# Tokens on partitions for the last expert sums: fp32 matmuls with the one-hots as stationary operand in place of two float32r passes, copies and transposes

## What is computed

```python
x = x + _L0_xattn_ref(_layernorm(x, axis=-1), ctx_1024, ...)
x = x + _L0_ffn_ref(_layernorm(x, axis=-1), L0_ffn_Wg, L0_ffn_W1, L0_ffn_W2)
...
expert_inputs = jnp.einsum('bnd,bnec->becd', token_inputs, dispatch)
h = jax.nn.gelu(jnp.einsum('becd,edh->bech', expert_inputs, W1))
expert_outputs = jnp.einsum('bech,ehd->becd', h, W2)
output = jnp.einsum('becd,bnec->bnd', expert_outputs, combine)
```

## Time and profile before

| | |
|---|---|
| median of 3 runs | 138.56 us (138.42 to 139.27) |
| the profiled execution | 138.64 us |
| its span | 136.9 us |
| busy in the span | PE 124.2 us (91%), DVE 93.6 us (68%), ACT 79.4 us (58%), POOL 33.6 us (25%) |
| granted TensorE clock, mean | 0.996 |

### The profile page before, as it was taken

One profiled execution on the slowest core, in us unless ns is written; L12 is line 12 of the kernel. 1 busy time (PEld: TensorE's weight loads), 2 busy tenths in 40 slices (PEclk: granted clock), 3 DMA queues, 4 the chain that ended last, 5 costly groups with the idle time before them and its releaser, 6 DMA issues.

```text
span 136.9 us, 2770 instructions
## 1 busy us (share of the span) xinstructions
PE 124.2 (91%) x1038; PEld 89.0 (65%) x1039; DVE 93.6 (68%) x304; ACT 79.4 (58%) x154; POOL 33.6 (25%) x54
## 2 busy tenths in 40 slices
PE   6999988999899998998978997699999999999950
PEld 2573843664664754754834943599999799987830
DVE  2797656996996996996997899974782041134751
ACT  1568383945855865765636678863694265315350
POOL 7633805005005005005000060027000065550000
PEclk9999999999999999999999999999999999999998
DMA  3989991000000000000000000000101201113115
GB/s 98 277 226 333 366 382 51 0 0 7 0 0 0 0 5 0 0 2 0 5 0 0 0 0 0 0 5 0 41 5 38 77 24 30 34 31 87 34 42 153
DMA packets 9197, 8.05 MB, mean 59 GB/s; under 512 B 601, under 2 KB 7028, under 8 KB 9184
## 3 DMA queue, kind: packets, MB, share of 16 engines
q1 hardware_dynamic: 8492, 7.28, 16.6%
q0 software_dynamic: 256, 0.40, 1.2%
q10 hardware_dynamic: 436, 0.20, 0.6%
HBM read 6.43 MB, written 1.57 MB: 58 GB/s over the span
## 4 chain that ended last, share of the span: by engine, by line
PE 71%; DVE 14%; ACT 9%; issue 3%; POOL 1%; ACTq 0%; DVEq 0%
PE ps L1302 11%; PE ps L1288 11%; PE ps L1144 6%; PE ps L1117 6%; PE ps L1136 5%; PE ps L1110 5%; PE ps L980 3%; PE ps L1314 3%; PE ps L1218 3%; ACT r_b L422 3%; PE ps L1063 3%; PE ps L1181 2%; PE ps L1093 2%; ACT z_b L436 2%; PE ps L1074 2%
## 5 line engine op out<-in xcount | busy, mean ns | idle before, releaser
L1144 PE MATMUL ps<-attn,VW 32*128 32x256 f32 x144 | 12.9, 426 | 3.5 <-DVE ps L712 2.0
L1288 PE MATMUL ps<-h,W_t 128*128 128x128 f32 x128 | 15.9, 279 | 0.0
L1288 PEld LDWEIGHTS ps<-h,W_t 128*128 128x128 f32 x128 | 15.0, 192 | 0.5 <-issue 0.3
L429 ACT ACTIVATE ps<-ps,half_b 128x512 f32<-128x512 f32 x12 | 7.9, 660 | 12.7 <-PE ps L1117 12.7
L1136 PE MATMUL ps<-h,whhT 128*128 128x256 f32 x48 | 13.7, 405 | 0.0
L1117 PE MATMUL ps<-h,whhT 128*128 128x256 f32 x48 | 13.3, 398 | 0.0
L346 POOL DMA_INDIRECT y_tok<-y_rows,row_of x8 | 8.3, 1034 | 18.9 <-DMA y_rows<-y_sb 14.1
L1144 PEld LDWEIGHTS ps<-attn,VW 32*128 32x128 f32 x144 | 5.6, 182 | 10.6 <-DVE ps L712 4.4
L1110 PE MATMUL ps<-h,whhT 128*128 128x256 f32 x48 | 11.7, 384 | 0.0
L422 ACT ACTIVATE r_b<-ps,half_b 128x512 f32<-128x512 f32 x12 | 7.6, 684 | 7.1 <-PE ps L1144 7.1
L712 DVE SCALAR_TENSOR_TENSOR ps<-r_b,ps 128x512 f32<-128x512 f32 x12 | 7.8, 693 | 5.1 <-ACT r_b L422 5.1
(11 more groups left out here) (168 smaller groups left out, 255.2 us busy)
## 6 DMA issues: line engine op xcount, KB each, us to landing
W_t<-in_L_ffn_W_dram SPq DMA_DIRECT2D x1, 2048.0 KB, 9.6
x_tok<-in_x_dram SPq DMA_DIRECT2D x4, 256.0 KB, 3.9
out_dram<-h SPq DMA_DIRECT2D x4, 256.0 KB, 2.3
y_rows<-y_sb SPq DMA_DIRECT2D x4, 128.0 KB, 1.8
n_b<-in_L_xattn_gru_whh_dram SPq DMA_DIRECT2D x1, 192.0 KB, 4.1
n_b<-in_L_xattn_gru_wih_dram SPq DMA_DIRECT2D x1, 192.0 KB, 3.5
y_tok<-y_rows,row_of POOLq DMA_INDIRECT x8, 3.7
n_b<-in_ctx_dram ACTq DMA_DIRECT2D x1, 64.0 KB, 2.9
```

The costliest lines, as they stand in the source:

```text
L1144: last = mm(to[:, hf, :], VW[g][p:p + M, gate * P:(gate + 1) * P], attn[g][p:p + M, :], start=False, stop=True, skip_group_check=True)
L1288: last = mm(hid_bank[e][:, j * BG * CAP:(j + 1) * BG * CAP], W1_t[:, ex_, j * P:(j + 1) * P], rhs, start=True, stop=True)
```

## The change

The combine of batches 2 and 3 is turned round. The one-hot of a piece of 128 tokens becomes the stationary operand and y the moving one, so the sums come out with tokens on partitions. Both operands are fp32, where there were two float32r parts: ACT's `y_late_out` copies y once, and `y_low` is gone. A step has 2 batches x 4 pieces = 8 matmuls of 128 columns. The sums lie in four banks, two pieces to a bank, and `accD` now counts banks (four in all), each as soon as its second piece is done in step 7. `summed_out`, DVE's copy, `back`, ACT's gates and the final add of batch 3 are left out; DVE's `gated_out` reads the four banks directly for both batches. The output of batch 3 is written by two DMAs of half the size.

```diff
-        comb = [sb(f"comb{k}", [P, B, N], f32r) for k in range(2)]
+        comb = [sb(f"comb{k}", [P, BG, N]) for k in range(2)]
-        y_hi = sb("y_hi", [P, 2, B, D], f32r)
-        y_lo = sb("y_lo", [P, 2, B, D], f32r)
+        y_late = sb("y_late", [P, 2, BG, D])
...
-        acc_bank = [bank[4], bank[5]]
+        acc_bank = [[bank[4], bank[5]], [bank[0], bank[1]]]
...
-            for b in range(B):
-                sp.wait_ge(fin, (C, 2 * C, 3 * C, 3 * C + 1)[b])
+            for b in range(B - 1):
+                sp.wait_ge(fin, C * (b + 1))
...
-            sp.wait_ge(out_done, 16 * B)
+            for k in range(2):
+                cs = slice(2 * k, 2 * k + 2)
+                sp.wait_ge(fin, C * (B - 1) + 2 * k + 2)
+                sp.dma_start(out[B - 1].rearrange("(c p) d -> p c d", p=P)[:, cs, :],
+                             res[:, B - 1, :].rearrange("p (c d) -> p c d", d=D)[:, cs, :]).then_inc(out_done, 16)
+            sp.wait_ge(out_done, 16 * (B + 1))
...
-            def y_high(s):
+            def y_late_out(s):
                 act.wait_ge(yP, s + 1)
                 if s >= NP + 2:
                     act.wait_ge(accP, s - NP - 1)
-                nc.scalar.activation(y_hi[:, s % 2, 0:BG, :],
+                nc.scalar.activation(y_late[:, s % 2, :, :],
                                      y_bank[s % 2][:, 0:BG * D].rearrange("p (b d) -> p b d", d=D),
-                                     ACT.Copy).then_inc(yh, 1)
+                                     ACT.Copy).then_inc(yl, 1)
...
-            summed_out(2)
-            act.wait_ge(gt, 2)
-            act.wait_ge(backP, B - BG)
-            for c in range(C):
-                n = (B - 1) * C + c
-                nc.scalar.activation(oT[:, B - 1, c * P:(c + 1) * P], back_bank[B - 1][:, c * P:(c + 1) * P],
-                                     ACT.Copy, scale=gate[:, n:n + 1]).then_inc(go, 1)
...
             def gated_out(b):
-                dve.wait_ge(backP, b - BG + 1)
                 for c in range(C):
                     n = b * C + c
-                    v.scalar_tensor_tensor(out=res[:, b, c * D:(c + 1) * D], in0=back_bank[b][:, c * D:(c + 1) * D],
+                    dve.wait_ge(accD, (n - BG * C) // 2 + 1)
+                    v.scalar_tensor_tensor(out=res[:, b, c * D:(c + 1) * D], in0=acc_bank[b - BG][c // 2][:, c % 2 * D:(c % 2 + 1) * D],
...
-            dve.wait_ge(accD, BG)
-            v.tensor_copy(oT[:, B - 1, :], acc_bank[BG - 1][:, :]).then_inc(oTv, 1)
             dve.wait_ge(gt, 2)
-            gated_out(B - 2)
-            dve.wait_ge(go, C)
-            v.tensor_tensor(res[:, B - 1, :], oT[:, B - 1, :],
-                            x2_tok[:, (B - 1) * C:B * C, :].rearrange("p c d -> p (c d)"), ALU.add).then_inc(fin, 1)
+            gated_out(2)
+            gated_out(3)
...
-                    for part in (y_hi, y_lo):
-                        last = mm(acc_bank[i][:, :], part[:, s % 2, i, :], comb[s % 2][:, BG * g + i, :],
-                                  start=(k == 0 and part is y_hi), stop=(k == NP - 1 and part is y_lo))
-                    if k == NP - 1:
-                        last.then_inc(accD, 1)
-                    elif i == BG - 1:
-                        last.then_inc(accP, 1)
+                    for c in range(C):
+                        last = mm(acc_bank[i][c // 2][:, c % 2 * D:(c % 2 + 1) * D], comb[s % 2][:, i, c * P:(c + 1) * P],
+                                  y_late[:, s % 2, i, :], start=(k == 0 and c % 2 == 0), stop=(k == NP - 1),
+                                  skip_group_check=True)
+                        if k == NP - 1 and c % 2 == 1:
+                            last.then_inc(accD, 1)
+                if k < NP - 1:
+                    last.then_inc(accP, 1)
```

More of the change, by code:

```diff
@@ L177, in slot_attention_and_switch_ffn @@
         xe = h2[:, :, :].rearrange("p b n -> p (b n)").rearrange("p (e b c) -> p e b c", e=E, b=B)
-        oT = d_b
         res = h
@@ L200, in slot_attention_and_switch_ffn @@
         y_bank = [bank[6], bank[7]]
-        back_bank = [bank[0], bank[1], bank[2], bank[3]]
         x_in = sems("x_in", B)
@@ L227, in slot_attention_and_switch_ffn @@
             sem(n) for n in ("lgP", "lmx", "dl", "gl", "lx", "ls", "gt", "fi", "fm", "mk", "posP", "pl"))
-        dsp, xeP, xeC, srP, srC, cmb, hidP, hidC, yP, yh, yl, accP, accD, oTs, oTv, backP, go, fin = (
-            sem(n) for n in ("dsp", "xeP", "xeC", "srP", "srC", "cmb", "hidP", "hidC", "yP", "yh", "yl",
-                             "accP", "accD", "oTs", "oTv", "backP", "go", "fin"))
+        dsp, xeP, xeC, srP, srC, cmb, hidP, hidC, yP, yl, accP, accD, fin = (
+            sem(n) for n in ("dsp", "xeP", "xeC", "srP", "srC", "cmb", "hidP", "hidC", "yP", "yl",
+                             "accP", "accD", "fin"))
         block = ctx.enter_context(nc.Block())
@@ L558, in y_high @@
                     act.wait_ge(accP, s - NP - 1)
-                nc.scalar.activation(y_hi[:, s % 2, 0:BG, :],
+                nc.scalar.activation(y_late[:, s % 2, :, :],
                                      y_bank[s % 2][:, 0:BG * D].rearrange("p (b d) -> p b d", d=D),
-                                     ACT.Copy).then_inc(yh, 1)
-            def summed_out(b):
-                act.wait_ge(accD, b - BG + 1)
-                nc.scalar.activation(oT[:, b, :], acc_bank[b % BG][:, :], ACT.Copy).then_inc(oTs, 1)
+                                     ACT.Copy).then_inc(yl, 1)
             x2_out(2)
@@ L590, in _ @@
                     gate_exp(1)
-                y_high(s)
-            summed_out(2)
-            act.wait_ge(gt, 2)
-            act.wait_ge(backP, B - BG)
-            for c in range(C):
-                n = (B - 1) * C + c
-                nc.scalar.activation(oT[:, B - 1, c * P:(c + 1) * P], back_bank[B - 1][:, c * P:(c + 1) * P],
-                                     ACT.Copy, scale=gate[:, n:n + 1]).then_inc(go, 1)
+                y_late_out(s)
         @block.vector
@@ L904, in combine_hot @@
                     dve.wait_ge(srC, b - BG + 1)
-                    v.tensor_scalar(comb[s % 2][:, b, :], srow[:, b, :], pair_iota[:, k:k + 1], None,
+                    v.tensor_scalar(comb[s % 2][:, b - BG, :], srow[:, b, :], pair_iota[:, k:k + 1], None,
                                     ALU.is_equal).then_inc(cmb, 1)
[L908 to L914, removed]
             def source_rows(i):
@@ L952, in _ @@
             combine_hot(5)
-            y_low(4)
-            y_low(5)
             combine_hot(6)
@@ L957, in _ @@
             gated_rows(0)
-            y_low(6)
             combine_hot(7)
             gated_rows(1)
-            y_low(7)
             gates(1)
-            dve.wait_ge(accD, BG)
-            v.tensor_copy(oT[:, B - 1, :], acc_bank[BG - 1][:, :]).then_inc(oTv, 1)
             dve.wait_ge(gt, 2)
-            gated_out(B - 2)
-            dve.wait_ge(go, C)
-            v.tensor_tensor(res[:, B - 1, :], oT[:, B - 1, :],
-                            x2_tok[:, (B - 1) * C:B * C, :].rearrange("p c d -> p (c d)"), ALU.add).then_inc(fin, 1)
+            gated_out(2)
+            gated_out(3)
         @block.tensor
@@ L1363, in _ @@
             combine(7)
-            back(2)
-            back(3)
 _INS = ["x", "ctx_1024", "L0_xattn_Wq", "L0_xattn_Wk", "L0_xattn_Wv", "L0_xattn_gru_wih", "L0_xattn_gru_whh",
```

## The result

| | before | changed |
|---|---|---|
| median of 20 runs | 138.68 us (138.23 to 139.27) | 139.41 us (138.91 to 141.52) |
| ratio to the kernel before | | 1.005, 95% interval 1.0036 to 1.0064 |
| the profiled execution | 138.64 us, span 136.9 | 139.13 us, span 137.4 |

The change makes the kernel slower by half a per cent, 0.73 us. That is clear of noise with 20 runs each, and inside the 1% that the prediction called no change; 139.3 was forecast.

What follows compares the result with a forecast made beforehand. PE was taken as the bound, without slack from up(4) to combine(7). Combines +0.85, +0.86, +1.62 and a tail cut from 3.40 to 0.84 moved the last add +0.77; queued DMAs made it +0.66: 138.64 + 0.66 = 139.30, range 138.6 to 140.0.

Steps and rivals of the forecast that it cites:

- PE's price: Four fp32 combines on PE, records 0.111 apart: combine(4) +0.85, combine(5) +0.86, combine(6) and combine(7) together +1.62.
- the pair: combine(6) and combine(7) back to back on PE, 32 records: 3.83 from first start to last end, against 2.21 before.
- No slack on PE: Between up(4) and combine(7) PE has no idle time, so each microsecond added there moves the end.
- The covers: ACT's copy of y and DVE's one-hots finish while PE is busy with earlier work: cost nothing, smallest room 1.3.
- The tail: Engine work after PE's last matmul: shrinks from 3.40 to 0.84, with DVE's eight gated adds setting the end.
- The DMAs: Output transfers at the end: batch 2's and batch 3's halves queue behind each other, last landing at 137.16, +0.66.
- a transfer alone: Other end of the output estimate: the last half lands 1.8 after issue, unhindered by other transfers, at 136.77, +0.27.
- The sum: Whole kernel: profiled execution 138.64 + 0.66 = 139.30, leaving out the 0.08 by which the median lay below it.
- The slower pace: Rival on the 64 records of the four combines: 0.136 each as in the transposes, 140.7 us; chance of slower pace 0.12.
- the second price: Skill page's rule for 128-column matmuls that each load weights: 162 ns a record in the four combines, 142.4 us.
- the single-record rival: Rival: an fp32 one-hot matmul leaves one record, four combines take 4.4 as before, 136.3 us; chance 0.03.
- Absorbed time: Rival: waits before down(7) or combine(6) hide PE's added time, so combine(4) and combine(5) cost nothing, 137.6 us; chance 0.05.

Runs made afterwards that it cites:

- batch-by-batch order: Changed kernel with the last two combines ordered (6, batch 2), (7, batch 2), (6, batch 3), (7, batch 3): 138.77 us, ratio 1.0013.
- side by side: Changed kernel in float32r with y's high and low parts as one moving operand of 256 columns, sums in columns of their own: 138.57 us, ratio 0.9996.

## Why the prediction was right

*PE's price.* combine(4) to up(7) was forecast at 1.89 and is 122.37 - 120.48 = 1.89; combine(5) to down(7) 1.98 and is 1.98; the pair 3.83 and is 3.84. PE's last matmul was put at 134.10 and is at 133.87 + 0.24 = 134.11. The step that made this possible was to take the price from up, whose matmuls have the very form of the new ones. The fp32 arithmetic alone, in the old layout, costs 3.1; so with fp32 it is the arithmetic that costs, not the turn. The two float32r parts in the new layout (1.84 a step) cost as much, so a return to them would not have saved it.

*No slack on PE.* Leaving out 8 of the matmuls, worth 1.78, took 1.78 off the span from up(4) on, and 1.9 to 2.0 off the median, so nothing absorbs it.

*The covers.* combine_hot(7) is done at 129.12 against a need near 131.9, and no wait of PE for the one-hots or for y stands in its rows. Zero was right.

*The tail.* It was forecast at 0.84 and is 0.92. The 0.08 stands before the first gated add: PE's first bank is done at 133.87 - 3 x 0.445 = 132.54 and DVE starts at 132.63, 0.09 later instead of 0.04. That DVE and not PE sets the end is shown by its one block without a gap, and by the batch-by-batch order, in which PE ends at the same time, DVE waits between the batches, and the last add still comes 0.2 earlier.

*The DMAs.* The data of batch 2 and both halves take 0.275 + 0.505 + 0.5 + 0.475 + 0.05 = 1.8 of all engines' time by the stretches, where 1.84 was forecast, and run in one piece. Taking the split back cost 0.1, and bringing batch 2 forward cut the halves' landing from 2.2 to 1.8. So the value taken (+0.66) was the right one of the two ends and not the +0.27 of a transfer alone.

*The pieces together.* PE's combines cost 3.34 more (7.71 against 4.37), the tail behind PE shrinks by 2.48 (3.40 to 0.92), and the last DMA lands 0.1 sooner after its issue (2.3 to 2.2). That leaves 0.75 or so, against 0.74 from up(4) on.

*The sum.* +0.66 was forecast and the medians give 139.41 - 138.68 = +0.73. The profiled execution shows +0.49, because its front part was 0.24 shorter. The 0.08 between the profiled execution and the median of before was rightly left out of the sum: it belonged to a median of 3, and over 20 runs the median of before is 138.68.

*The rivals.* The slower pace (0.136 a record, 140.7) is excluded by the 0.111 of the rows, and so is the 162 ns of the second price on the Trainium skill's page "TensorE: Matmul & The Clock Gate", section "Back-to-back issue gap". (The section calls its first price, N/2.4 + 2.5 ns, the gap of an isolated matmul, not that of a stream; the rows lie at it all the same, 0.111 with 2 x 128 columns.) The rival's own price was misread: the 8 transposes in 1.22 include a wait, that of back(3) for DVE's copy, and two slow first steps of 0.17. Inside each group of four they stand 0.109 apart, no slower than up's records. So the row gave no ground for 0.136, nor for the 4.4 of the single-record rival, which would have been 32 x 0.109 = 3.5. Absorbed time is excluded by the experiment with half left out, and the single record by the 16 records of a combine.

*Where the gain went.* With one float32r pass the new form is 2.3 faster than the kernel before; some 0.4 of that is PE (0.95, 1.04 and 2.00 for the combines against 1.04, 1.12 and 2.21) and the other 1.9 is the new end. On PE, fp32 costs 3.06 more than the two float32r parts in the old layout, and 3.34 more with the new layout as well. Full precision at the old PE price exists in the new layout too (side by side), but there the second adds on DVE make the end as long as the old one. The change buys a shorter end with more PE time in four steps that all lie on the path.

## What to carry to other kernels

Price a new matmul from a row of the same form (size of both operands, type, a new stationary operand or not), from the steps inside a group and not from its total, which may hold a wait or a slow first step. For long operands count the streamed columns: at 512 columns an fp32 matmul cost four times a float32r one (some 0.9 against 0.23). For short ones look for a floor: with 128 stationary columns loaded for each record, no run of records here kept a step below 0.11. Where PE never waits, matmul time added in four steps adds up in full, while what it buys at the end is bounded by the next engine in line (DVE here) and then by the bytes of the output that stand in the queue together. A smaller last DMA lands sooner only when the transfer before it is already out of the way (1.8 against 2.2 here), so bring the earlier one forward first.

## What the runs showed of the hardware that was not expected

Within a group, fp32 and float32r matmul records with a load of 128 stationary columns each followed one another no faster than 0.11 us, however few columns they streamed. The step was 0.111 for an fp32 record with 128 columns (2 x 128 streamed, as worked out in the prediction), 0.109 in the transposes, and 0.111 to 0.112 in float32r with 128 columns, also where the next matmul had the same stationary operand. The router's matmuls (L1181 in the kernel before) show it best. They stream 8 columns only, and their 16 records still take (1.85 - 0.26 - 0.03) / 14 = 0.111 each behind a first step of 0.03:

```profile
76.51 1.85 PE L1181 MATMUL ps<-Wg_c,xT 128*128 128x8 f32 x16
```

The only shorter steps are first ones like that, where the loads run ahead of the matmuls (0.03 here, 0.06 in slot_rows). With 256 float32r columns most steps were 0.115 to 0.122 (the first of the 16 was 0.22 and the one into combine(7) 0.19). So halving the columns from 256 to 128 wins next to nothing, and a low part of 128 columns costs as much as an fp32 matmul's second record. With 512 columns in fp32 the loads hardly count: 8 records in 3.70 against 32 in 3.84 for the same columns. The Trainium skill's page "TensorE: Matmul & The Clock Gate", section "LDWEIGHTS (loading the stationary operand)", gives a weight load as its columns over 1.2 GHz, 107 ns for 128 columns. The traces agree with that as a floor for the spacing (0.109 to 0.112, but for such first steps), though the rows of the 128-column loads in up and combine themselves last 0.19 and overlap. For fp32 the loads and the 2 x 128 streamed columns would give nearly the same 0.11, so it is the float32r rows and the router's that tell that the load sets this floor.

An fp32 matmul with only 64 stationary columns cost half of one with 128. down's 16 matmuls take 1.90, and up's 8 take 1.98. down leaves two records a matmul as well, but they start 7 ns apart, and the next pair follows some 0.11 later.
